# A mixture-of-experts and attention kernel: the one-hot matrices of its token lists built as two wide fp16 products, finished on ACT, and read with a step of six

## What is computed

```python
scores = softmax(x @ gate_w.T)                    # [2048, 64]
topk_w, topk_ids = top_k(scores, 6)
comb = zeros(T, 64).at[arange(T)[:, None], topk_ids].add(topk_w / sum(topk_w))
gu = einsum('th,efh->tef', x, w_gate_up)          # the kernel computes chosen tokens only
act = silu(gu[..., :176]) * gu[..., 176:] * comb[:, :, None]
routed = einsum('tef,ehf->th', act, w_down)
out = x + attention(xn) + routed + shared(xn)
```

## Time and profile before

| | |
|---|---|
| time, median of 3 runs | 731.99 us (728.43 to 732.77) |
| the profiled execution | 725.61 us, span 723.8 us |
| granted TensorE clock, mean | 0.981 |
| busy | PE 93%, PEld 60%, DVE 69%, ACT 45%, POOL 55% |
| shared stage | about 77 to 158 us |
| 12 one-hot instructions of DVE for each of 16 token tiles | 192 in all, 69.9 to 133 us |
| 96 list matmuls | 80.6 to 136 us |

### The profile page before, as it was taken

The page is one execution under the profiler, slowest core; times in us unless marked ns, Lnnn a source line. Parts: engine busy times, 40 slices in busy tenths (PEclk is TensorE's granted clock), DMA queues, the critical chain, the costliest instruction groups (busy, mean ns, idle before and its releaser), DMA issues.

```text
span 723.8 us, 19510 instructions
## 1 busy us (share of the span) xinstructions
PE 674.7 (93%) x5200; PEld 434.2 (60%) x5202; DVE 497.2 (69%) x1184; ACT 326.6 (45%) x849; POOL 396.6 (55%) x383
## 2 busy tenths in 40 slices
PE   6899999989999999999999999999778998999996
PEld 3755677664555555555555555555456776677764
DVE  5498899856666666667666666656377779777751
ACT  2432322224444444444444444444446566656552
POOL 2000000227787777777787776763776776677520
PEclk9599999999999999999999999999989999999998
DMA  8500000037676766767676763342122312231310
GB/s 282 185 1 1 1 0 1 22 112 233 191 211 195 224 211 214 224 211 214 211 224 191 248 210 98 98 96 58 59 66 73 100 55 67 88 98 57 96 59 30
DMA packets 54288, 90.75 MB, mean 125 GB/s; under 512 B 8694, under 2 KB 32438, under 8 KB 54246
## 3 DMA queue, kind: packets, MB, share of 16 engines
q1 hardware_dynamic: 23494, 43.11, 19.9%
q0 software_dynamic: 10752, 29.37, 14.4%
q10 hardware_dynamic: 20000, 17.73, 7.3%
HBM read 69.21 MB, written 20.97 MB: 125 GB/s over the span
## 4 chain that ended last, share of the span: by engine, by line
PE 61%; DVE 9%; POOL 8%; DMA 7%; issue 6%; ACT 3%; DVEq 2%; SPq 2%; ACTq 1%; POOLq 0%
PE pair L1023 20%; PE pair L1058 10%; PE pair L933 6%; POOL wqkv_sb L436 5%; DMA lower<-wdn 5%; PE pair L1009 4%; PE bank L1032 3%; PE pair L1042 3%; PE bank L996 3%; DMA wqkv_sb<-y_rows,slot_i 3%; PE bank L1134 2%; DVE negm L829 2%; DVE space L806 2%; POOL space L432 2%; PE bank L1081 1%
## 5 line engine op out<-in xcount | busy, mean ns | idle before, releaser
L380 POOL DMA_INDIRECT lower<-xn_rows,idx_all x128 | 136.9, 1069 | 228.4 <-DVE idx_all L752 135.5
L1023 PE MATMUL pair<-space,work 128*64 (+1 forms) x768 | 166.0, 463 | 7.9 <-DMA lower<-wdn 3.3
L1058 PE MATMUL pair<-lower,work 88*64 x512 | 121.6, 379 | 1.3 <-ACT work L537 1.0
L1023 PEld LDWEIGHTS pair<-space,work 128*64 128x64 f32 x768 | 66.9, 136 | 80.3 <-issue 56.5
L522 ACT ACTIVATE work<-pair 128x176 f32<-128x176 f32 x160 | 51.5, 322 | 117.4 <-PE pair L1023 59.9
L1058 PEld LDWEIGHTS pair<-lower,work 88*64 88x64 f32 x512 | 69.6, 137 | 48.1 <-issue 11.2
L762 DVE TENSOR_TENSOR work<-work,pair 128x176 f32<-128x176 f32 x160 | 53.1, 333 | 60.5 <-ACT work L522 60.0
L812 DVE COPY space<-lower 88x512 f32 x64 | 78.8, 1231 | 22.2 <-issue 21.8
L1023 PE MATMUL pair<-wqkv_sb,work 128*64 128x352 f32 x256 | 89.4, 472 | 0.0
L529 ACT ACTIVATE lower<-pair 128x256 f32<-128x256 f32 x128 | 49.3, 385 | 77.7 <-PE pair L1058 77.7
L557 ACT ACTIVATE pT<-pair 128x768 f32<-128x768 f32 x64 | 52.0, 812 | 58.9 <-PE pair L1121 56.2
(11 more groups left out here) (171 smaller groups left out, 1346.9 us busy)
## 6 DMA issues: line engine op xcount, KB each, us to landing
space<-wgu SPq DMA_DIRECT2D x66, 352.0 KB
y_rows<-lower ACTq DMA_DIRECT2D x128, 128.0 KB
lower<-wdn SPq DMA_DIRECT2D x66, 176.0 KB
x_all<-x SPq DMA_DIRECT2D x4, 512.0 KB, 7.7
xn_rows<-qk_all SPq DMA_DIRECT2D x16, 128.0 KB, 2.0
lower<-xn_rows,idx_all POOLq DMA_INDIRECT x128
out<-x_all SPq DMA_DIRECT2D x8, 256.0 KB, 2.5
wqkv_sb<-wqkv SPq DMA_DIRECT2D x1, 768.0 KB, 12.5
```

Of the source, the lines that this page charges most:

```text
L380: po.indirect_dma_start(xg[:, r % XB, :], None, xn_rows[:, :], bass.IndirectOffsetOnAxis(idx_all[:, r:r + 1], 0)).then_inc(xg_in[r % XB], 16)
L1023: last = pe.matmul(pair[u % 2][strip, 0:2 * F], xgT[u][:, c, strip], n, start=c == 0, stop=c == EC - 1, skip_group_check=True)
L1058: last = pe.matmul(pair[u % 2][strip, 512:512 + E], hT[:, u % 2, c, strip], n, start=c == 0, stop=c == 1, skip_group_check=True)
```

## The change

The six choices of a token tile come to lie side by side, as the innermost dimension of `is_row`, `is_tile` and `iota_b`. DVE then makes each matrix of all six with one `tensor_tensor` over 768 fp16 values; `slot_row` and `slot_tile` are fp16 now and are read with their six values again for each of the 128 positions. The token's number is no longer multiplied in by DVE but by ACT, in place, in a new function `token_numbers(t)`. The list matmuls read both operands at every sixth column. The wait of PE is on ACT's result now, and LIST_LAG is 3.

```diff
-LIST_LAG = 2
+LIST_LAG = 3
...
-        slot_tile = sb("slot_tile", [P, NT, 8])
-        slot_row = sb("slot_row", [P, NT, 8])
+        slot_tile = sb("slot_tile", [P, NT, 8], F16)
+        slot_row = sb("slot_row", [P, NT, 8], F16)
...
-        iota_b = sb("iota_b", [P, RT], F16)
+        iota_b = sb("iota_b", [P, P, TOPK], F16)
...
-        with nc.sbuf_tensor("is_row", [P, 2, TOPK, P], F16) as is_row, \
-                nc.sbuf_tensor("is_tile", [P, 2, TOPK, RT], F16) as is_tile:
+        with nc.sbuf_tensor("is_row", [P, 2, P, TOPK], F16) as is_row, \
+                nc.sbuf_tensor("is_tile", [P, 2, RT, TOPK], F16) as is_tile:
...
+            def token_numbers(t):
+
+                act.wait_ge(onehot_raw, t + 1)
+                act.activation(is_tile[:, t % 2], is_tile[:, t % 2], ACT.Copy, scale=tok_sb[:, t:t + 1]).then_inc(onehot_ok, 1)
+
             def first_tiles(i):
+                for t in range(NT):
+                    if max(LIST_AT[t] + 1, t - 2) == i:
+                        token_numbers(t)
...
-            dve.tensor_copy(iota_b[:], iota_f[:, 0:RT])
+            dve.tensor_copy(iota_b[:], iota_f[:, 0:RT].unsqueeze(2).to_broadcast([P, RT, TOPK]))
...
-                for k in range(TOPK):
-                    dve.tensor_scalar(is_row[:, u, k], iota_b[:], slot_row[:, t, k:k + 1], None, ALU.is_equal)
-                    last = dve.tensor_scalar(is_tile[:, u, k], iota_b[:], slot_tile[:, t, k:k + 1], tok_sb[:, t:t + 1],
-                                             ALU.is_equal, ALU.mult)
-                last.then_inc(onehot_ok, 1)
+                dve.tensor_tensor(is_row[:, u], iota_b[:], slot_row[:, t, 0:TOPK].unsqueeze(1).to_broadcast([P, P, TOPK]),
+                                  ALU.is_equal)
+                dve.tensor_tensor(is_tile[:, u], iota_b[:], slot_tile[:, t, 0:TOPK].unsqueeze(1).to_broadcast([P, RT, TOPK]),
+                                  ALU.is_equal).then_inc(onehot_raw, 1)
...
-                    mm = pe.matmul(listed_at, is_row[:, t % 2, k], is_tile[:, t % 2, k], start=t == 0 and k == 0,
+                    mm = pe.matmul(listed_at, is_row[:, t % 2, :, k], is_tile[:, t % 2, :, k], start=t == 0 and k == 0,
```

More of the change, by code:

```diff
@@ L232, in build @@
         tiled = sem("tiled"); placed = sem("placed"); passed_ok = sem("passed_ok"); ended = sem("ended")
-        tables_ok = sem("tables_ok"); onehot_ok = sem("onehot_ok"); listed = sem("listed"); idx_ok = sem("idx_ok"); dpair = sem("dpair")
+        tables_ok = sem("tables_ok"); onehot_raw = sem("onehot_raw"); onehot_ok = sem("onehot_ok"); listed = sem("listed"); idx_ok = sem("idx_ok"); dpair = sem("dpair")
         w_loaded = [sem("w_loaded_even"), sem("w_loaded_odd")]
```

## The result

The changed kernel takes 743.78 us (median of six runs, 739.59 to 744.82) against 732.34 us for the kernel before on the same chip (six runs, 728.43 to 734.2). The ratio is 1.0158 with a 95% interval of 1.0122 to 1.0194: slower by 1.6%, or 11.6 us (8.9 to 14.2). The forecast of 731 and the range to 739 both missed it. The profiled execution took 742.68 us, with a span of 740.9 and a mean granted clock of 0.968.

What follows compares the result with a forecast made beforehand. PE was taken as the bound, with 1.4 us of waits for DVE in the shared stage. Terms -1.4 + 0.2 + 96 x 0 = -1.2 us on the 732.0 median gave 730.8, said as 731; range 726 to 739.

Steps and rivals of the forecast that it cites:

- 96 x 0: Shared stage: 96 list matmuls reading operands 12 bytes apart on PE were priced at 0 extra ns each.
- 0, 53 and 168 ns: Extra per list matmul: as now, at the fp32 transposes' pace, or at the fp32 up's (0.225 us for 128 columns).
- rival 2: Strided list reads make the kernel slower, from 89 ns extra each; needs fp32-up pace or unhidden weight loads; 747 at 168; chance 0.12.
- no longer hide: List matmuls: weight loads not covered by a 57 ns matmul, the second way rival 2 could come true.
- The Trainium skill's rule: SBUF is read in 16-byte lines; at least two reads must share one; spoke against 12-byte steps, gave no price.
- -1.4 us, PE's waits for DVE: Shared stage: PE waits 1.4 us in all for DVE's late one-hots, and all of it goes.
- DVE's one-hots at 0.93: Shared stage: a `one_hot` falls from 2.32 to 0.93 us, as 2-byte operands go two at a time.
- ACT's pass at 0.85: Shared stage: each of 16 in-place passes over 768 values takes 0.85 us and holds up no later `silu`.
- The 0.2 us charged at the start: First list of the shared stage: ACT's first pass, behind the first `silu`, may delay PE; 0 to 0.2, taken as 0.2.
- The lag at nothing: Shared stage: `one_hot(t)` waits for `list_tokens(t-2)` in the same step; table one step (2.3 us) later, covered, so no cost.
- Whatever the shared stage gains or loses passes on in full, and nothing else in the kernel is touched: Behind the shared stage: routed loads start when the last up ends, so later stages only shift by its gain or loss.

Runs made afterwards that it cites:

- weights alone at step 6: Changed kernel, but only the weights, `is_row`, read at every sixth column, with the moving side `is_tile` contiguous; ratio to the kernel before 1.0056.
- contiguous: Changed kernel with both one-hots stored choice by choice again, so list matmuls read both operands contiguously; ratio to the kernel before 1.0044.
- step-2 kernel: Changed kernel with the choices in three groups of two, so both operands are read at a step of 2 values (4 bytes); ratio 1.0034.
- step 2 with memsets: The step-2 kernel plus 160 one-element DVE memsets where DVE idles for the router's logits; ratio to the kernel before 0.9996.

## Why the prediction was wrong, point by point

**PE's strided operands: the term "96 x 0".** This is the step that failed. It said that nothing in the trace showed that a 12-byte step costs passes. In fact a product went from 57 to 173 ns, 117 more (by 0.70 / 6), and 96 x 0.117 = 11.2 us. The mechanism had been named and bounded from both sides (0, 53 and 168 ns), and the choice of the lower end was made from the absence of a row, which is no evidence. The measured value lies between the middle row and the upper one. It is above the 89 ns from which rival 2 decides, so rival 2, given 0.12, is what happened. Of its two reasons the first, slow reads, is right in kind, though 173 ns is short of the fp32 up's 225; the second, weights that "no longer hide", is wrong, and the kernel with weights alone at step 6 shows it. The prediction also lumped two operands into one price although they use PE in different ways.

The Trainium skill's rule, quoted ahead ("Advanced Engine Details and Errata", section "SBUF Cachelines"), pointed the right way for the moving operand, and the measured 173 ns agrees with its direction. It also covers cases where the measurement differs: steps of 3 still put more than two reads on a line on average (48 lines for 128 reads) and cost 31 ns, and weights at step 6 cost nothing that is waited for. The measurement decides there.

**-1.4 us, PE's waits for DVE.** Right. No wait is left in 81.4 us, and the contiguous and step-2 kernels, with PE's products back at 57 ns, have a shared stage 1.0 to 1.2 us shorter. The sum for the changed kernel's stage closes: -1.4 + 11.2 = 9.8, less 16 x 0.05 for the up behind a list, which is 1.19 instead of 1.24, makes 9.0. The trace has 86.9 - 77.7 = 9.2.

**DVE's one-hots at 0.93.** Right in mechanism: two values at a time. The instructions are 558 and 551 ns long; 0.54 was expected.

**ACT's pass at 0.85.** It is 0.92; neither row used was SBUF in fp16. Harmless, as computed: with it alone the routed loop and the shared stage lose nothing, and that kernel is at 0.9989 (0.9958 to 1.0021). The 0.2 us charged at the start are not there: from the first `silu` in the chain to the first list it is 81.03 - 79.84 = 1.19 us, against 80.74 - 79.57 = 1.17 in the earlier trace rows, and transposes stand right ahead of the list.

**The lag at nothing.** Right for the changed kernel (86.9 against 87.0 us). Alone, in the kernel before, it would have cost 2.1 us.

**"Whatever the shared stage gains or loses passes on in full, and nothing else in the kernel is touched".** The first half fits the totals, as closely as the scatter of the gap and the rest lets one tell. The second failed: the routed loop is 4.2 us longer, in every kernel of the study that has 144 to 160 DVE instructions fewer ahead of it and no memsets in their place. This term was missing from the sum and no rival had it. The trace of before holds the copies that POOL's instructions stretch to 1.8 us, a sign that DVE's timing matters there, but not the 0.1 us gaps.

**The sum as it should have been.** -1.4 - 0.8 + 11.2 + 4.2 = +13.2 us, inside the interval of 8.9 to 14.2. For the step-2 kernel: -1.0 + 3.8 = +2.8, and the ratio gives 2.5. For the changed kernel with 160 memsets: 9.3 - 0.2 = +9.1, and the ratio gives 10.4 (7.4 to 13.4).

**No version beats the kernel before.** The two best are before with ACT's pass (0.9989) and step 2 with memsets (0.9996), and both intervals hold 1. The 1.0 us that they gain in the shared stage is less than these runs can tell.

**What stays open.** What DVE's sequencer does in the 0.10 us behind the branch and at the place that repeats; whether that place comes every 256 or every 128 instructions; where PE's stage behind the loop loses its 7 to 12 us, and whether by the same cause; and why the clock falls in the gap in one execution and not in another of the same kernel.

## What to carry over

Price the two operands of a matmul apart. A moving operand that is read at every sixth fp16 value triples a 128-column product, while pairs side by side give DVE its faster pace and cost PE nothing. Where the trace has no row for an operand's form on the engine that sets the end, the absence of a row doesn't speak for the lower bound. And after an edit that changes how many instructions an engine has, cut both traces by stages: a stage that was not edited can move by 1% for that reason alone, and some idle instructions in an engine's spare time show whether it is that. Then lay the same pass of a loop side by side in both traces: where the loop's passes have two lengths, look for the first instruction that is late.

## What the runs showed of the hardware

- PE, fp16, moving operand of 128 columns: 57 ns contiguous, 58 at a 4-byte step, 88 at 6 bytes, 173 at 12 (at 4 and 6 bytes the weights were strided too). Stationary operand at 12 bytes: load 125 ns instead of 97, and no longer list group (0.34 us).
- DVE, fp16 `tensor_tensor` over 768 values: 558 ns when two or six values are repeated side by side, 956 when one value is repeated 128 times in a row.
- ACT, fp16 in place on SBUF, 768 values, scale from a column: 924 ns.
- DVE, one-value memset: 59 ns.
- DVE's sequencer, loop of 66 instructions: 0.24 instead of 0.14 us between the branch back and the next instruction, and 0.10 us more at one place inside, where a place that comes every 256 (or 128) instructions lies in the loop; ten traces of 19.
- DVE's fp32 copy of 88x512: 0.42 us alone; where POOL starts a `TENSOR_TENSOR` during it, up to 2.1 us, ending 0.3 us after POOL's instruction (31 copies in the kernel before, 41 in the changed).
- Routed loop 338.7 to 339.7 us or 343.0 to 343.8 by DVE's number of instructions ahead (once 341.3); the part behind it 215.2 to 220.4, or 227.0 to 227.7 with 192 more on PE.
- Start of the routed stage, 14.1 us at a granted clock of 1.00, 19.1 at 0.77.
